# Spreading the FP4 weight quantising step by step over the second expert layer, and moving up tiles and down groups ahead of the transposes that end a token norm

## The reference

```python
x = x + tanh(g_xattn[n]) * attention_n(layernorm(x), ctx, ctx)
x = x + tanh(g_ffn[n]) * ffn_n(layernorm(x))
```

```python
nx  = ln(x) * g + b
w   = softmax(nx @ router_w), top 2 kept and normalised
h1  = gelu(nx @ up_W[e])                        # 128 -> 512, each expert
s0  = gelu(ln(h1[e] @ spec0_W))                 # experts 0, 4: 512 -> 512
s1  = ln(gelu(h1[e] @ spec1a_W) @ spec1b_W)     # experts 1, 5: 512 -> 256 -> 512
s2  = gelu(h1[e] @ spec2_W)                     # experts 2, 6: 512 -> 512
                                                # experts 3, 7: h1 as it is
y   = sum over e of w[e] * (h2[e] @ down_W[e])
```

## Time and profile before

| | us |
|---|---|
| runs of the kernel before | 744.95, 742.23, 742.43 (median 742.43) |
| the profiled execution | 743.6 |
| its span in the profile | 741.9 |
| PE busy in the span | 668.3 (90%) |
| DVE busy | 477.2 (64%) |
| ACT busy | 437.2 (59%) |
| POOL busy | 182.5 (25%) |
| mean granted PE clock | 0.958 |

### The profile page before, as it was taken

How to read it: one execution, slowest core, us unless ns; L and a number is a source line. 1 busy time by engine, 2 the same in 40 slices (tenths; PEclk the granted TensorE clock), 3 DMA queues, 4 the chain that set the end, 5 groups by cost and what they waited for, 6 DMA issues and landing times.

```text
span 741.9 us, 10203 instructions
## 1 busy us (share of the span) xinstructions
PE 668.3 (90%) x3566; PEld 488.7 (66%) x3575; DVE 477.2 (64%) x1093; ACT 437.2 (59%) x819; POOL 182.5 (25%) x215
## 2 busy tenths in 40 slices
PE   5889999997798898898989988998799997889997
PEld 1589996564466666676767776766464664667775
DVE  2477675585447567547554765476994863569996
ACT  4356454876436658657358485544226673887873
POOL 3414000540124041223341512024002101124531
PEclk9989999999789999999999999997999999899999
DMA  5112002020002000102020110010000100110001
GB/s 136 48 30 61 1 1 72 1 86 2 0 3 79 5 15 29 59 13 85 15 64 9 53 33 0 1 47 0 1 1 12 47 3 0 29 29 29 1 0 29
DMA packets 27361, 20.98 MB, mean 28 GB/s; under 512 B 5409, under 2 KB 22571, under 8 KB 27311
## 3 DMA queue, kind: packets, MB, share of 16 engines
q1 hardware_dynamic: 26591, 20.29, 9.2%
q10 hardware_dynamic: 720, 0.04, 0.1%
HBM read 19.80 MB, written 0.52 MB: 27 GB/s over the span
## 4 chain that ended last, share of the span: by engine, by line
PE 65%; DVE 20%; ACT 7%; issue 4%; POOL 2%; DMA 1%; ACTq 0%; DVEq 0%; POOLq 0%
PE PS L1457 57%; PE PS L1697 3%; PE PS L1563 2%; ACT XN L746 1%; DVE SN L1137 1%; DVE ST L1011 1%; PE PS L1614 1%; PE PS L1719 1%; DVE H2l L1179 1%; DVE H1l L1179 1%; POOL WL L642 1%; ACT H1h L836 1%; ACT PS L839 1%; DMA GW<-in_L_gate_T 1%; PE PS L1478 1%
## 5 line engine op out<-in xcount | busy, mean ns | idle before, releaser
L642 POOL TENSOR_TENSOR WL<-RAW,WH 128x512 fp32r<-128x512 f32 (+2 forms) x76 | 89.3, 1191 | 152.9 <-ACT WH L730 152.5
L1179 DVE TENSOR_TENSOR H2l<-PS,H2h 128x512 fp32r<-128x512 f32 x72 | 48.9, 688 | 63.1 <-ACT PS L839 62.8
L730 ACT ACTIVATE ATT<-PS 77x512 f32<-77x512 f32 (+5 forms) x92 | 46.9, 534 | 39.8 <-PE PS L1890 15.7
L634 POOL TENSOR_TENSOR RSTD<-VE,MHALF 128x4 f32<-128x4 f32 x18 | 18.4, 1024 | 200.5 <-DVE VE L1021 164.8
L1457 PE MATMUL PS<-H1h,WH 128*128 128x512 f32 x146 | 61.4, 421 | 6.9 <-DVE H1l L1179 6.9
L1457 PE MATMUL PS<-XTh,WH 128*128 128x512 f32 x128 | 53.8, 420 | 11.8 <-DVE XTl L1039 5.7
L660 POOL TENSOR_TENSOR XT<-XT,YW 128x512 f32<-128x512 f32 x24 | 32.2, 1344 | 118.2 <-DVE YW L1116 118.2
L1457 PE MATMUL PS<-H1l,WH 128*128 128x512 f32 x146 | 58.5, 401 | 0.0
L1457 PE MATMUL PS<-H1h,WL 128*128 128x512 f32 x146 | 58.2, 399 | 0.0
L1457 PE MATMUL PS<-XTh,WL 128*128 128x512 f32 x128 | 52.5, 410 | 0.0
L1457 PE MATMUL PS<-XTl,WH 128*128 128x512 f32 x128 | 52.3, 409 | 0.0
(11 more groups left out here) (251 smaller groups left out, 1681.2 us busy)
## 6 DMA issues: line engine op xcount, KB each, us to landing
RAW<-in_L_ffn_spec_W SPq DMA_DIRECT2D x4, 1024.0 KB, 5.6
RAW<-in_L_ffn_w SPq DMA_DIRECT2D x16, 256.0 KB, 3.0
RAW<-in_L_ffn_up_W SPq DMA_DIRECT2D x8, 256.0 KB, 2.8
RAW<-in_L_ffn_down_W SPq DMA_DIRECT2D x8, 256.0 KB, 3.3
RAW<-in_L_ffn_spec1a_W SPq DMA_DIRECT2D x2, 512.0 KB, 4.4
RAW<-in_L_ffn_spec1b_W SPq DMA_DIRECT2D x2, 512.0 KB, 6.1
RAW<-in_L_ffn_wg SPq DMA_DIRECT2D x4, 176.0 KB, 2.6
RAW<-in_L_ffn_wu SPq DMA_DIRECT2D x4, 176.0 KB, 2.6
```

Of the source, the lines that this page charges most:

```text
L634: step(g.tensor_tensor(RSTD[:, c], VE[:, c], MHALF[:, c], ALU.pow))
L642: g.tensor_tensor(lo, RAW[0:r["rows"], r["raw"] + s["c0"]:r["raw"] + s["c1"]], hi.bitcast(fp32), ALU.subtract).then_inc(lo_done, 1)
L730: return s.activation(o, i, ACT.Copy)
L1179: v.tensor_tensor(lo, full, hi.bitcast(fp32), ALU.subtract).then_inc(split_done, 1)
```

## The change

Two edits, both in the order of the second expert layer. No instruction is added or taken away.

- The seven `quantise` steps become 63 steps (seven blocks of nine instructions), each one instruction. They no longer stand in e2 and e6; behind every `down` group of experts 2 and later (8 for each expert) stand the next two. The 63rd step is alone behind the 32nd group, `down` e5 half 1 i3.
- For e0 and e4 the first `up` tile of the next expert goes ahead of the first `turn` of half 1. For e1 and e5 `up` i2 of the next expert and the first two `down` groups of half 0 do, and within the weave a `down` group comes ahead of its `turn`.

```diff
@@ -158,7 +158,7 @@
     o = order[1]
     u, s = up(0, 0), group("spec0", 1, 0, 0, TH)
     o += u[0:1] + chain("late_scale") + u[1:2] + chain("late_stats") + u[2:4] + chain("late_norm") + s[0:2] + second
-    wq = [dict(kind="quantise", layer=1, i=i) for i in range(7)]
+    wq = [dict(kind="quantise", layer=1, i=i, k=k) for i in range(7) for k in range(9)]
     for e in range(E):
         spec = lambda kind, h, n, **m: group(kind, 1, e, h, n, **m)
         nxt = up(e + 1, 0) if e + 1 < E else []
@@ -172,30 +172,35 @@
             new = strips(E0P + e + 1)
         if e % 4 == 2 and e + 2 < E:
             new = new + strips(E0P + e + 2, ("inner",))
-        q = []
-        if e in (2, 6):
-            q, wq = wq[:4], wq[4:]
         if e % 4 == 0:
             o += weave(s[2:] if e == 0 else spec("spec0", 0, TH), up(e, 1), new[:4])
             k = route() if e == 0 else []
             o += k[0:1]
             o += weave(spec("spec0", 1, TH), spec("turn", 0, 4, buf=2, hi="act"), new[4:], k[1:])
-            o += weave(spec("turn", 1, 4, buf=3, hi="act"), down(e, 0), nxt[:2])
+            o += nxt[:1] + weave(spec("turn", 1, 4, buf=3, hi="act"), down(e, 0), nxt[1:2])
             o += weave(nxt[2:], down(e, 1))
         elif e % 4 == 1:
             o += weave(spec("spec1a", 0, 2, buf=2, hi="act"), up(e, 1), new[:3])
             o += weave(spec("spec1b", 0, TH), spec("spec1a", 1, 2, buf=3, hi="act"), new[3:])
             o += weave(spec("spec1b", 1, TH), spec("turn", 0, 4, buf=2, hi="act"), nxt[:2])
-            o += weave(spec("turn", 1, 4, buf=3, hi="act"), down(e, 0), nxt[2:3])
+            o += nxt[2:3] + weave(down(e, 0), spec("turn", 1, 4, buf=3, hi="act"))
             o += weave(nxt[3:], down(e, 1))
         elif e % 4 == 2:
-            o += weave(spec("spec2", 0, 4, buf=2, hi="act"), up(e, 1), new[:2], q[:2])
-            o += weave(spec("spec2", 1, 4, buf=3, hi="act"), down(e, 0), new[2:], q[2:])
+            o += weave(spec("spec2", 0, 4, buf=2, hi="act"), up(e, 1), new[:2])
+            o += weave(spec("spec2", 1, 4, buf=3, hi="act"), down(e, 0), new[2:])
             o += weave(nxt, down(e, 1))
         else:
             o += weave(up(e, 1), new)
             o += down(e, 0)
             o += weave(nxt, down(e, 1))
+
+    spread_out = []
+    for s in order[1]:
+        spread_out.append(s)
+        if s["kind"] == "down" and s["e"] >= 2:
+            spread_out += wq[:2]
+            wq = wq[2:]
+    order[1] = spread_out + wq
 
     x = [(e, h) for e in range(E) for h in range(2)]
     for n in range(len(x) + 2):
@@ -1146,7 +1151,7 @@
                     elif kind == "second":
                         low_of_xt(n, (1,))
                     elif kind == "quantise":
-                        quantise_weights(i)
+                        quantise_weights(i, s["k"])
                     elif kind == "gate_up":
                         bank = ring_bank(layer, j + 1)
                         k = s["dve"] - 1
@@ -1306,24 +1311,34 @@
                         first_half_normed(i - (TH * NG + WEIGH_LAG - 2))
                 settle()
 
-            def quantise(src, n, parts=128, scratch=None):
+            def quantise_step(k, src, n, parts=128, scratch=None):
 
                 nb = n // QB
                 p = slice(0, parts)
                 blk = lambda x: x.rearrange("p (b k) -> p b k", k=QB)
                 per = lambda i: QS[p, i, 0:nb].rearrange("p (b o) -> p b o", o=1).to_broadcast([parts, nb, QB])
-                now(v.tensor_reduce(QS[p, 0, 0:nb], blk(src), AX.X, ALU.max, apply_absolute_value=True))
-                now(v.tensor_scalar(QS[p, 0, 0:nb], QS[p, 0, 0:nb], 1.0 / 6.0, 1e-12, ALU.mult, ALU.max))
-                now(v.reciprocal(QS[p, 1, 0:nb], QS[p, 0, 0:nb]))
                 m, q = (x[p, 0:n] for x in (scratch or (QA, QC)))
-
-                now(v.scalar_tensor_tensor(blk(m), blk(src), 1.0 - 2.0 ** -23, per(1), ALU.mult, ALU.mult))
-
-
-                now(v.tensor_scalar(q.bitcast(u32), m.bitcast(u32), 0x7F800000, None, ALU.bitwise_and))
-                now(v.tensor_scalar(q, q, 1.5 * 2.0 ** 22, 1.5 * 2.0 ** 22, ALU.mult, ALU.max))
-                now(v.tensor_tensor(m, m, q, ALU.add))
-                now(v.tensor_tensor(m, m, q, ALU.subtract))
+                if k == 0:
+                    now(v.tensor_reduce(QS[p, 0, 0:nb], blk(src), AX.X, ALU.max, apply_absolute_value=True))
+                elif k == 1:
+                    now(v.tensor_scalar(QS[p, 0, 0:nb], QS[p, 0, 0:nb], 1.0 / 6.0, 1e-12, ALU.mult, ALU.max))
+                elif k == 2:
+                    now(v.reciprocal(QS[p, 1, 0:nb], QS[p, 0, 0:nb]))
+                elif k == 3:
+                    now(v.scalar_tensor_tensor(blk(m), blk(src), 1.0 - 2.0 ** -23, per(1), ALU.mult, ALU.mult))
+                elif k == 4:
+                    now(v.tensor_scalar(q.bitcast(u32), m.bitcast(u32), 0x7F800000, None, ALU.bitwise_and))
+                elif k == 5:
+                    now(v.tensor_scalar(q, q, 1.5 * 2.0 ** 22, 1.5 * 2.0 ** 22, ALU.mult, ALU.max))
+                elif k == 6:
+                    now(v.tensor_tensor(m, m, q, ALU.add))
+                else:
+                    now(v.tensor_tensor(m, m, q, ALU.subtract))
+
+            def quantise(src, n, parts=128, scratch=None):
+
+                for k in range(8):
+                    quantise_step(k, src, n, parts, scratch)
 
             def scaled_back(dst, n, parts=128, scratch=None):
                 nb = n // QB
@@ -1333,20 +1348,24 @@
                 scale = QS[p, 0, 0:nb].rearrange("p (b o) -> p b o", o=1).to_broadcast([parts, nb, QB])
                 return v.tensor_tensor(blk(dst), blk(m), scale, ALU.mult)
 
-            def quantise_weights(i):
-
-                if i == 0:
+            def quantise_weights(i, step):
+
+                if i == 0 and step == 0:
                     dve.wait_ge(in_w2, 16 * len(LAYER2))
                 if i < 6:
                     k = min(128, I2 - 128 * (i % 3))
                     w = W2R[0:k, i // 3, i % 3, :]
-                    quantise(w, D, k, W2S)
-                    now(scaled_back(w, D, k, W2S))
+                    if step < 8:
+                        quantise_step(step, w, D, k, W2S)
+                    else:
+                        now(scaled_back(w, D, k, W2S))
                 else:
                     w = W2R[:, 2, :, :].rearrange("p c k -> p (c k)")[:, 0:I2]
-                    quantise(w, I2, 128, W2S)
-                    scaled_back(w, I2, 128, W2S).then_inc(wq_ready, 1)
-                    dve.wait_ge(wq_ready, 1)
+                    if step < 8:
+                        quantise_step(step, w, I2, 128, W2S)
+                    else:
+                        scaled_back(w, I2, 128, W2S).then_inc(wq_ready, 1)
+                        dve.wait_ge(wq_ready, 1)
 
 
             dve.wait_ge(in_x, 16)
```

## The result

The change makes the kernel faster, by about a third of what was forecast. Median of 9 runs 739.12 us (736.72 to 740.40), before 742.43 us (9 runs, 740.30 to 744.95); the ratio is 0.9945, 95% interval 0.9927 to 0.9962, some 4.1 us (the medians themselves lie 3.3 apart). The forecast was 731.4 with a range of 727.5 to 737.0. The profiled execution took 737.75 us (span 736.0), 5.85 less than the profiled one of before; that pair lies further apart than the medians do.

What follows compares the result with a forecast made beforehand. TensorE was taken to bound the kernel; 4.0 + 4.3 - 1.3 + 4.0 - 1.7 - 0.1 + 0.3 + 1.5 = 11.0 us off the profiled 743.6, adjusted to the median, gave 731.4 us, range 727.5 to 737.

Steps and rivals of the forecast that it cites:

- the 4.0, 4.3 and 4.0 of the sum: Gains in us forecast from moving the quantising out of e2's first half, e2's second half and e6.
- The two terms of 4.0: e2's first half and e6: wait of 3.03 us falls to 0.7 and 1.7 of half clock goes, 4.0 us each.
- The 4.3: e2's second half: gain of 4.3 us once the quantising block and the 2.38 us wait are gone.
- its 4.75: e2's second half: 18 matmuls end 4.75 us earlier, before 0.45 is taken off for a late low part.
- e0's term: e0: filling the norm wait gains 0, the routing wait grows to 3.0 us and half clock follows, -1.7 us.
- the signs named: Included norm waits gone at e0, e1, e4, e5, and a wait of about a microsecond before e4's inner product.
- the ceiling: Second expert layer: at most 29.7 us to gain, 23.7 of TensorE idle time plus 6 of half clock.
- I take -1.3: e3: steps and GpSimd holds delay the last low part before e4's inner product, costing 1.3 us (0 to 1.3).
- DVE falls behind: Rival at e3: steps and holds make a 5.0 us wait, half clock of 1.7 follows; 736.8 us, chance 0.12.
- -1.7 - 0.1 + 0.3 + 1.5: The second edit's terms in us for filling the norm waits at e0, e1, e4 and e5.
- bound of 0.5% for faster: Whole kernel: 0.5%, 3.7 us, is about what measurement can tell from no change; faster means under 738.7.
- the working had said of e1: e1: filling the 1.92 us norm wait gains nearly nothing, as ACT works unbroken and TensorE waits in half 1; -0.1.

Runs made afterwards that it cites:

- e2: Not a run: expert 2 of the second expert layer, a place in the kernel.
- e6: Not a run: expert 6 of the second expert layer, a place in the kernel.
- d: The change with the same 63 steps behind the down groups of experts 4 to 7 instead of 2 to 5; 738.65 us, ratio to before 0.9938.
- f: The change with expert 0's order put back and the steps behind the down groups of experts 3 to 6; 731.29 us, ratio to before 0.9843.
- g: The change with expert 0's order put back and three steps behind each down group of experts 4 to 6; 732.52 us, ratio to before 0.9861.
- j: The change without its second edit, steps behind the down groups of experts 3 to 6; 729.71 us, ratio to before 0.9823.
- k: The change with expert 0's order put back and no steps behind the down groups of e2's second half; 731.87 us, ratio to before 0.9847.
- b: The kernel before with the second edit alone (reordering), quantising still in blocks of nine; 745.80 us, ratio to before 1.0041.
- c: The change with expert 0's order alone put back, its up tile after the first transposes again; 733.80 us, ratio to before 0.9877.
- i: The change with the two middle parts of the routing moved earlier at expert 0; 736.01 us, ratio to before 0.9895.
- a: The kernel before with the first edit alone, single steps behind the down groups of experts 2 to 5; 737.72 us, ratio to before 0.9919.

## Why the prediction was wrong, by its steps

**What held.** The quantising blocks were the cause of the waits at e2 and e6, and taking them away gave 3.93, 3.79 and 3.92 us for the 4.0, 4.3 and 4.0 of the sum. The two terms of 4.0 were right in both parts, the wait (0.71 and 0.70 left, 0.7 forecast) and the clock behind it. A small wait in front of it is in both kernels and changes nothing; before it read

```profile
312.63 0.50 PE L1457 MATMUL PS<-H1h,WH 128*128 128x512 f32 x1 [0.41 <-DVE H1l L1179]
```

and after it is the row at 314.47. The 4.3 was 0.5 too large: it took 0.45 off its 4.75 for a late low part, and the change's own steps in that half cost 0.95. In the five kernels without them there (d, f, g, j, k) the stretch gains 4.73 or 4.74, the full 4.75 of the working. Some 1.6 us of it is the half clock, which did not fall there in b. e0's term had the right mechanism, "3.0 is nearest to 3.03: -1.7": the wait was 3.00 and the clock fell. It lasted 6.0 us, not 3.4, so the term was 2.8. The ledger's e1, e4 and e5 are within 0.3 of the sum. Of the signs named, two did not come: 1.09 us is left of the norm waits at e0 and e4, as their own working of 0.7 us filled implies, and the wait in e3 to e4 stands at another matmul. One reading was wrong without touching the sum: a mean clock of 0.96 over 300 us is 12 us of lost time, not 6, so the ceiling was some 36 us, not 29.7.

**The step that failed is e3, "I take -1.3".** It looked for the price in the low part that e4's inner product needs, bounded between 0 and 1.3. DVE's backlog was real, and steps beside GpSimd's pieces did take 1.0 to 1.3 us. But the first to be late was the *weighing*, a DVE instruction in the same queue. GpSimd reads it, and GpSimd's next work is the weights of e4's first up tile. That path needs no low part of a hidden tile. The working counted DVE's queue for one reader only and took GpSimd's pieces as fixed in time, while they are fixed only in order. The price was 2.02 of wait and 1.7 of half clock, 3.84 in all. Against a kernel without the eight steps, which loses 0.65 to 0.69 there, the steps cost about 3.2 us at this place and 0.95 in e2's second half. The rival "DVE falls behind" (736.8) priced the place at 6.7, too much, and had the same wrong matmul; it was given 0.12.

The rule cited from the Trainium skill (SBUF — State Buffer, Who interferes with whom) would have brought e3's price near 0 by letting short steps come first. The rows show the reverse order ahead of the first weighing: the steps at 329.94 and 331.19 lie within GpSimd's pieces, which had started at 328.52, and were held. Even where a step came unheld it was not free, since its own time stands in DVE's queue ahead of the weighing. GpSimd's pieces took 1.27 us each as before, and no row here shows one held by a step.

**The time outside the layer.** The profiled execution of before lay 1.2 us over its median and that of the change 1.4 under, so 5.85 us between profiles is 3.3 between medians and 4.1 by the ratio. The layer's 6.1 us is what two single executions show; the medians show less. Behind the layer the mean granted clock was 0.95 in the profiled execution of before and 0.93 or 0.94 in those of the change, b, c, i and j, and that stretch took 249.2 us before and 249.5 to 252.9 in these. Whether this is chance or follows from the changed layer is not settled. By the ratio the result lies just beyond the prediction's bound of 0.5% for faster, by the median just short of its 738.7.

**The second edit was misjudged as a whole.** The sum gave it 0: -1.7 - 0.1 + 0.3 + 1.5. Alone it costs 3.0 us by time, 1.0 in the layer; within the change its four places sum to -1.7 in the ledger, and a's layer is 1.7 the shorter. And its one gain, 1.25 at e5, was half clock that did come behind a wait of 1.95 us in the kernel before and in a, and did not in j. Without it, f against j says that filling norm waits gives nothing: the time comes back as waits for low parts that stand behind ACT, as the working had said of e1.

**What stays open.** What makes the clock fall is not settled by the length of the wait ahead of it. It fell behind every wait of 3.0 us (e0, e2, e6) and behind each of 2.0 us at e4's first tile; it never fell behind 2.3 us at e0 or 1.9 at e1, and behind 2.4 at e2 and 1.95 at e5 it fell in some kernels and not in others. Nothing was tried that keeps a wait on purpose and changes what surrounds it.

## What to carry to other kernels

When short steps are dealt out into an engine's slack, list every reader of that engine behind them, also those that reach the bound engine by way of a third one; here eight steps ahead of one weighing cost some 4 us. Put them where the next instruction in the queue is needed last, and not in the last stretch before a hand-over, where they cost 4.5 us.

Work put into a wait pays only if the wait behind it does not grow: an up tile moved ahead by 0.7 us made the next wait 3.0 us, brought 6 us of half clock and cost 2.8. Measure a change's two edits apart; here the first alone, with its steps started an expert later, is about 9 us better than the two together.

## What was not expected

- Waits of nearly the same length, at the same place, were followed by half clock in one kernel and not in another: 2.38 in the kernel before, 2.40 in b; 1.95 in the kernel before, 1.95 in j. A term for the clock had better be carried as a chance than as a sum.
- A half clock behind a wait of 3.0 us lasted 3.4 us at e2 and e6 and 6 us at e0. No run here shows why.
- The gain of c over the change, 5.3 us, is larger than its layer shows (2.85); the part outside is not explained by any row here.
